# The causal mask mostly inside the second score product and the maxima product, mask products of 64 and 65 columns

## The reference

```python
q = apply_rotary_emb(q, cos, sin)
k = apply_rotary_emb(k, cos, sin)
scores = jnp.einsum('bhid,bhjd->bhij', q, k) * scale
scores = jnp.where(causal, scores, -jnp.inf)
probs = jax.nn.softmax(scores, axis=-1)
out = jnp.einsum('bhij,bhjd->bhid', probs, v)
```

## Time and profile before

| | |
|---|---|
| median of 3 runs | 1208.22 us (1207.09 to 1208.79) |
| profiled execution, its own time | 1207.18 us |
| its span in the trace | 1205.1 us |
| PE busy | 1128.8 us, 94% of the span, 13543 matmuls |
| DVE / ACT / POOL busy | 994.7 / 939.9 / 938.7 us |
| slots 1 to 14 in the trace | 130.1 to 896.0 us |
| last slot | to about 950 us, then the feed-forward part |

### The profile page before, as it was taken

How to read it: one execution, slowest core, us unless ns; L and a number is a source line. 1 busy time by engine, 2 the same in 40 slices (tenths; PEclk the granted TensorE clock), 3 DMA queues, 4 the chain that set the end, 5 groups by cost and what they waited for, 6 DMA issues and landing times. The chain is left out here.

```text
span 1205.1 us, 34913 instructions
## 1 busy us (share of the span) xinstructions
PE 1128.8 (94%) x13543; PEld 790.1 (66%) x13543; DVE 994.7 (83%) x2262; ACT 939.9 (78%) x2180; POOL 938.7 (78%) x980
## 2 busy tenths in 40 slices
PE   4689999999999999999999999999998788999996
PEld 1256677777767777777777777777776555566563
DVE  7799797888879797978879797879789579877987
ACT  3667988889797979789797979788898576656574
POOL 3468899999999999999989999999677445334463
PEclk8699999999999999999999999999999899999999
DMA  6651524262442515252534515152520100000011
GB/s 204 160 141 47 131 65 116 69 141 68 110 116 63 140 38 143 69 125 63 133 85 94 132 46 141 47 132 72 141 68 2 36 1 2 1 2 1 2 36 36
DMA packets 50660, 97.03 MB, mean 81 GB/s; under 512 B 6720, under 2 KB 23360, under 8 KB 48448
## 3 DMA queue, kind: packets, MB, share of 16 engines
q1 hardware_dynamic: 50496, 94.81, 31.5%
HBM read 58.47 MB, written 34.60 MB: 77 GB/s over the span
## 5 line engine op out<-in xcount | busy, mean ns | idle before, releaser
L847 POOL TENSOR_TENSOR Plo<-P,Phi 128x512 f16<-128x512 f32 (+3 forms) x640 | 538.1, 868 | 69.9 <-ACT P L516 66.7
L513 ACT ACTIVATE Phi<-psS 128x512 f16<-128x512 f32 (+3 forms) x768 | 392.5, 511 | 131.2 <-PE psS L368 83.2
L516 ACT ACTIVATE P<-psS 128x512 f32<-128x512 f32 (+3 forms) x640 | 315.1, 493 | 0.0
L392 PE MATMUL psO<-V,Plo 128*128 128x65 f16 x2304 | 288.4, 194 | 0.0
L388 PE MATMUL psO<-V,Phi 128*128 128x65 f16 x2304 | 287.1, 192 | 0.3 <-DVE On L805 0.3
L390 PE MATMUL psO<-V,Phi 128*128 128x64 f16 x2304 | 286.2, 192 | 0.0
L365 PE MATMUL psS<-Q,K 128*128 128x512 f16 (+3 forms) x768 | 251.6, 328 | 12.6 <-DVE Plo L672 9.5
L388 PEld LDWEIGHTS psO<-V,Phi 128*128 128x128 f16 x2304 | 219.7, 98 | 56.7 <-issue 1.0
L368 PE MATMUL psS<-Q,K 65*128 65x512 f16 (+3 forms) x768 | 252.3, 329 | 0.0
L721 DVE TENSOR_REDUCE pmax<-psX 128x1 f32<-128x512 f32 x384 | 242.8, 682 | 1.1 <-PE psX L452 0.6
L390 PEld LDWEIGHTS psO<-V,Phi 128*128 128x128 f16 x2304 | 213.9, 96 | 30.8
(11 more groups left out here) (194 smaller groups left out, 2175.8 us busy)
## 6 DMA issues: line engine op xcount, KB each, us to landing
K<-k_way SPq DMA_DIRECT2D x48, 512.0 KB, 6.9
k_way<-HL SPq DMA_DIRECT2D x64, 256.0 KB, 4.2
q_way<-HL SPq DMA_DIRECT2D x60, 256.0 KB, 3.9
Q<-q_way SPq DMA_DIRECT2D x60, 256.0 KB, 6.8
Q<-q_way SPq DMA_DIRECT2D x15, 512.0 KB, 11.7
out<-y SPq DMA_DIRECT2D x8, 256.0 KB, 2.2
y<-in_x SPq DMA_DIRECT2D x3, 512.0 KB, 10.9
Q<-HL SPq DMA_DIRECT2D x16, 64.0 KB, 4.8
```

What stands on the lines that cost most here:

```text
L392: mm = nc.tensor.matmul(O, M.Plo[:, U % NP_, k * P:(k + 1) * P], V[:, HD:2 * HD + 1], start=False, stop=j == t, skip_group_check=True)
L513: nc.scalar.activation(M.Phi[:, U % NP_, 0:w], X, ACT.Exp, scale=SCALE)
L516: nc.scalar.activation(full, X, ACT.Exp, scale=SCALE).then_inc(S.exp_done, 1)
L847: nc.gpsimd.tensor_tensor(M.Plo[:, U % NP_, 0:w], M.P32[:, U % NP_, 0:w], M.Phi[:, U % NP_, 0:w], ALU.subtract).then_inc(S.lo_pool, 1)
```

## The change

The idle rows 65 to 127 of `K2` and `Q2` get a constant pattern: row r of `K2` holds 32768 at key r of each block and 0 elsewhere, row r of `Q2` holds -32768 at the queries below r. Their product is a large negative number where the key is above the query, for keys 65 to 127 of a block. So the diagonal 128 columns are a product of all 128 rows, the other columns one of 65 rows, and a mask product is left for keys 0 to 64 alone: 64 query columns in the scores, 65 key columns in the maxima. The 65-row operands are now high against high: `K2` holds key high and `Q2` query high, `K1` key low and key high, `Q1` query high and query low. The maxima are taken from `K2` and `Q2` alone, without the term of the low keys, and row 64 of `Q2` is zeroed by a DMA ahead of them. The pattern is built by POOL in `Plo` and copied by ACT (16 copies of 64 x 1024 f16, `far_rows`) during the start. Two small DVE copies become reductions. `load(s)` still moves 3 MB in 8 DMAs, the first one being the row of zeros of 8 KB. The DMA of the row of 64.0 and its semaphore go.

```diff
 NEG = -1.0e30
 LOWEST = -3.0e38
 MSCALE = 64.0
+BIG = 32768.0
+LEFT = HD + 1
 VW = 2 * HD + 2
 E, TOPK, H = 8, 4, 128
 SH = 2 * H
 assert sorted((t, j + i) for bank in MAXB for t, j, n in bank for i in range(n)) == [
     (t, j) for t in range(TT) for j in range(t + 1)]
 LO_LAG = 0
+NEAR = (48, 32)
 LAG = 5
 NP_ = 6
 NS = 3
 MT_FIRST = ((-1, 17), (0, 1), (0, 11), (0, 19))
 MX_SECOND, JOIN_SECOND, MT_SECOND = (13, 41), 42, 44
 EARLY_STEPS = 12
+FAR_AT = {(-2, 2): (4, 5), (-2, 3): (6, 7), (-2, 6): (8, 9), (-2, 8): (10, 11), (-1, 20): (12, 13), (-1, 22): (14, 15)}
 X_SUM = {(-2, 8): 1, (-2, 10): 2, (-1, 2): 3}
 X_SQUARE = {(-1, 5): (1, 2), (-1, 17): (3,)}
 X_ROOT, X_RECIPROCAL = (-1, 19), (0, 6)
...
                 nc.tensor.matmul(out, M.K1[:, p, h, j * P:(j + 1) * P], M.Q1[:, p, h, c:c + w],
                                  start=True, stop=False)
 
-                mm = nc.tensor.matmul(out, M.K2[0:HD + 1, p, h, j * P:(j + 1) * P],
-                                      M.Q2[0:HD + 1, p, h, c:c + w], start=False, stop=not diagonal)
+                keys = slice(j * P, (j + 1) * P)
                 if diagonal:
-                    mm = nc.tensor.matmul(out[:, 0:P], M.ident16[:], M.maskT[:], start=False, stop=True)
+                    nc.tensor.matmul(out[:, 0:P], M.K2[:, p, h, keys], M.Q2[:, p, h, keys], start=False, stop=False)
+                    if w > P:
+                        nc.tensor.matmul(out[:, P:w], M.K2[0:LEFT, p, h, keys], M.Q2[0:LEFT, p, h, c + P:c + w],
+                                         start=False, stop=False)
+                    mm = nc.tensor.matmul(out[:, 0:HD], M.ident16[:], M.maskT[:], start=False, stop=True)
+                else:
+                    mm = nc.tensor.matmul(out, M.K2[0:LEFT, p, h, keys], M.Q2[0:LEFT, p, h, c:c + w],
+                                          start=False, stop=True)
                 mm.then_inc(S.scores_ready, 1)
 
             def weighted(U):
...
                                                   start=i == 0, stop=i == 2)
                 elif kind == "mx":
                     h, k = a
-                    if (s, h, k) == (-1, 1, 0):
-                        pe.wait_ge(S.first_twin, 16)
+                    if (s, h, k) == (-1, 0, 0):
+                        pe.wait_ge(S.far_rows, 2 * GH)
+                    if (s, h, k) == (0, 0, 0):
+                        pe.wait_ge(S.far_rows, 4 * GH)
                     if k == 0 and h % 2 == 0:
                         if s < 0:
                             pe.wait_ge(S.first_k, 32)
                             pe.wait_ge(S.first_q[h // 2], 16 * GH)
                         else:
-                            pe.wait_ge(S.near_in[h // 2], 48 * (s + 1))
+                            pe.wait_ge(S.near_in[h // 2], NEAR[h // 2] * (s + 1))
                     c = 0
-                    rows = HD if s < 0 and h == 0 else P
                     for t, j, n in MAXB[k]:
                         diagonal = j + n - 1 == t
-                        mm = nc.tensor.matmul(X[:, c:c + n * P], M.Q1[0:rows, p, h, t * P:(t + 1) * P],
-                                              M.K1[0:rows, p, h, j * P:(j + n) * P], start=True, stop=not diagonal)
-                        c += n * P
+                        plain = n - diagonal
+                        own = slice(t * P, (t + 1) * P)
+                        if plain:
+                            mm = nc.tensor.matmul(X[:, c:c + plain * P], M.Q2[0:LEFT, p, h, own],
+                                                  M.K2[0:LEFT, p, h, j * P:(j + plain) * P], start=True, stop=True)
+                        c += plain * P
                         if diagonal:
-                            mm = nc.tensor.matmul(X[:, c - P:c], M.ident16[:], M.maskN[:], start=False, stop=True)
+                            nc.tensor.matmul(X[:, c:c + P], M.Q2[:, p, h, own], M.K2[:, p, h, own],
+                                             start=True, stop=False)
+                            mm = nc.tensor.matmul(X[:, c:c + LEFT], M.ident16[:], M.maskN[:], start=False, stop=True)
+                            c += P
...
+            def far_rows(n):
+
+                p, k, h = n // (2 * GH), n // GH % 2, n % GH
+                rows = (M.K2, M.Q2)[k][HD:P, p, h].rearrange("p (t i) -> p t i", i=P)
+                pattern = M.Plo[HD:P, k, 0:P].rearrange("p (o i) -> p o i", o=1)
+                nc.scalar.copy(rows, pattern.to_broadcast([HD, TT, P])).then_inc(S.far_rows, 1)
+
...
+            act.wait_ge(S.patterns, 2)
+            for n in range(2):
+                far_rows(n)
             for k in range(2):
                 tiles = slice(k * HT, (k + 1) * HT)
                 act.wait_ge(S.var_ready[0], k + 1)
                 nc.scalar.activation(M.std[:, tiles], M.std[:, tiles], ACT.Sqrt).then_inc(S.std_ready[0], 1)
+            for n in range(2, 4):
+                far_rows(n)
             weight_hi(0)
             for s, u in steps:
                 U = SU * s + u
                 if s >= 0 and U <= last_unit:
                     exps(U)
+                for n in FAR_AT.get((s, u), ()):
+                    far_rows(n)
                 for item in act_at.get((s, u), []):
                     side(item)
...
-                nc.vector.tensor_copy(M.pmax[:, 1, h, 0:5:4], M.pmix[:, h, 0:2, 3]).then_inc(S.max_parts, 1)
+                nc.vector.tensor_reduce(M.pmax[:, 1, h, 0:5:4], M.pmix[:, h, 0:2, 3:4], AX.X, ALU.max).then_inc(S.max_parts, 1)
...
-                nc.vector.tensor_copy(M.pmax[:, 1, :, 0:5:4], M.pmix[:, :, 0:2, 3]).then_inc(S.max_parts, 1)
+                nc.vector.tensor_reduce(M.pmax[:, 1, :, 0:5:4], M.pmix[:, :, 0:2, 3:4], AX.X, ALU.max).then_inc(S.max_parts, 1)
...
             nc.gpsimd.memset(M.ident[:], 0.0)
             nc.gpsimd.memset(M.ident16[:], 0.0)
             nc.gpsimd.memset(M.maskT[:], 0.0)
-            nc.gpsimd.memset(M.maskN[:], 0.0).then_inc(S.consts, 1)
+            nc.gpsimd.memset(M.maskN[:], 0.0)
+            nc.gpsimd.memset(M.Plo[:, 0, 0:P], 0.0)
+            nc.gpsimd.memset(M.Plo[:, 1, 0:P], -BIG).then_inc(S.consts, 1)
             pool.wait_ge(S.consts, 1)
             for t in (M.ident, M.ident16):
                 nc.gpsimd.affine_select(out=t[:], in_=t[:], compare_op=ALU.not_equal, fill=1.0, base=0,
                                         pattern=[[-1, P]], channel_multiplier=1)
 
+            nc.gpsimd.affine_select(out=M.Plo[:, 0, 0:P], in_=M.Plo[:, 0, 0:P], compare_op=ALU.not_equal, fill=BIG, base=0,
+                                    pattern=[[-1, P]], channel_multiplier=1)
+            nc.gpsimd.affine_select(out=M.Plo[:, 1, 0:P], in_=M.Plo[:, 1, 0:P], compare_op=ALU.is_ge, fill=0.0, base=-1,
+                                    pattern=[[-1, P]], channel_multiplier=1).then_inc(S.patterns, 1)
+
             nc.gpsimd.affine_select(out=M.maskT[:], in_=M.maskT[:], compare_op=ALU.is_ge, fill=NEG, base=0,
-                                    pattern=[[1, P]], channel_multiplier=-1)
+                                    pattern=[[1, HD]], channel_multiplier=-1)
             nc.gpsimd.affine_select(out=M.maskN[:], in_=M.maskN[:], compare_op=ALU.is_ge,
-                                    fill=NEG, base=0, pattern=[[-1, P]], channel_multiplier=1).then_inc(S.consts, 1)
-            nc.gpsimd.memset(M.scale_row[:], MSCALE)
+                                    fill=NEG, base=0, pattern=[[-1, LEFT]], channel_multiplier=1).then_inc(S.consts, 1)
+            pool.wait_ge(S.patterns, 1)
+            for k, value in enumerate((MSCALE, 0.0)):
+                last = nc.gpsimd.affine_select(out=M.Plo[:, k, 0:P], in_=M.Plo[:, k, 0:P], compare_op=ALU.not_equal,
+                                               fill=value, base=-HD, pattern=[[0, P]], channel_multiplier=1)
+            last.then_inc(S.patterns, 1)
+            nc.gpsimd.memset(M.zeros[:], 0.0)
             nc.gpsimd.memset(M.eps[:], EPS)
             nc.gpsimd.memset(M.V[:, :, :, :, 2 * HD:2 * HD + 1].rearrange("p a t h o -> p (a t h) o"), 1.0)
             nc.gpsimd.memset(M.pmax[:], LOWEST).then_inc(S.consts, 1)
...
                                  M.HL[h * HALF:(h + 1) * HALF, 0, :, :]).then_inc(S.first_out, 16)
                 sp.wait_ge(S.first_out, 16 * GH)
                 for i in range(2):
-                    sp.dma_start(M.K1[:, 0, 2 * i:2 * i + 2], krows[:, 2 * i:2 * i + 2]).then_inc(S.first_k, 16)
-                sp.dma_start(M.K2[0:HD, 0], krows[0:HD]).then_inc(S.first_k2, 16)
+                    sp.dma_start(M.K2[0:HD, 0, 2 * i:2 * i + 2], krows[0:HD, 2 * i:2 * i + 2]).then_inc(S.first_k, 16)
+                sp.dma_start(M.K1[0:HD, 0], krows[HD:P]).then_inc(S.first_k1, 16)
+                sp.dma_start(M.K1[HD:P, 0], krows[0:HD]).then_inc(S.first_k1, 16)
 
             def first_queries():
 
...
                 for h in range(GH):
                     rows = slice(h * HALF, (h + 1) * HALF)
                     for k in range(2):
```

(21 more changed lines are left out.)

27 lines of the change are left out of this document (12 added, 15 removed).

## The result

The changed kernel takes 1199.24 us (median of 6 runs, 1197.42 to 1203.23) against 1208.47 for the kernel before on the same chips (6 runs, 1205.76 to 1210.03): a ratio of 0.9927, 95% interval 0.9907 to 0.9948. It is faster by 9 us, and the forecast was 16. The profiled execution has a span of 1196.8 us against 1205.1, at a mean granted clock of 0.98.

What follows compares the result with a forecast made beforehand. PE was taken to bound slots 1 to 14. Gains of 20.5 us, less 2.8 give-back and 1.6 start, leave 16.1 off 1207.2: 1191.1, as median 1192; own range 1186 to 1197, widened to 1186 to 1199.

Steps and rivals of the forecast that it cites:

- the start: Before slot 1: ACT's pattern copies and a second table load, less DVE's saved copies, cost a net 1.6 us.
- masks: PE's mask products in scores and maxima: narrowing saves 0.027 us each, 1.73 us per slot.
- splits: PE's diagonal products cut in two: 48 more matmuls a slot at 0.007 us, 0.34 us in all.
- give-back: Slots 1 to 14: waits on other engines return 0.2 us of PE's saving per slot, 2.8 us in all.
- 0.7 for slot 0: Slot 0: gains half of a steady slot's 1.39 us, 0.7 us.
- I let 0.8 of them lie on its path: DVE's L744 copies at the start: some 2 us saved, 0.8 counted as lying on DVE's path.
- the price of 0 for the loads: Operand loads: same 3 MB and 8 issues, arriving earlier for the maxima and as before for the scores, cost 0.
- A: Steady slots: POOL and the three banks of scores hold the slot near 53.9 us; gain 6.3 us, 1202; chance 0.14.
- B: Start: costs +4 us in place of +1.6, the copies' delay running through DVE's slot 0; 1194.5; chance 0.14.
- C: PE's splits: switching active rows exposes the next weight load, 98 ns per split, 71 us; slower at 1253; chance 0.03.
- D: PE's masks: a 64-column bf16 product takes as long as one of 128, so no gain; 1215; chance 0.03.
- The test I set: Steady slots of the changed profile: forecast 53.0 to 53.2 us; staying above 53.6 would mean the forecast is wrong.

Runs made afterwards that it cites:

- `wide_masks`: The changed kernel with both mask products, of scores and maxima, 128 columns wide as before; 1210.87 us against 1208.51 for the kernel before.
- `before_less_act`: The kernel before, with ACT's exponentials on 448 of 512 columns in 16 units of a slot; 1198.42 us against 1208.51 for the kernel before.
- `no_masks`: The changed kernel without its mask products in the scores and the maxima; 1193.91 us against 1207.26 for the kernel before.
- `less_pool`: The changed kernel with POOL forming the low half of only 448 of 512 columns in 16 units of a slot; 1197.75 us against 1207.26 before.

## Why the prediction failed by half

**The step that failed** is the term "I take 0.2 us in each of 14 slots, nearer to 0, since no wait of more than 0.7 us is there today". A steady slot gave back 1.34 - 0.52 = 0.82 us. The range for it (0 to 0.9) held the value; the choice inside it did not. With 0.82 in place of 0.2 the sum would have been 8.7 us smaller and the forecast 1200.7, beside 1199.24 measured. That this is so near is in part luck: the start came out 1.2 us better than forecast, slots 9, 10 and 13 gained 1.7 us more than a steady slot, and slot 14 gave 1.6 back.

The range was also stated too narrow. With the ends that the prediction gives for each term (masks 0.030 and 0.024, splits 0 and 0.01, give-back 0 to 6, start -0.5 to 2.5), all at once, the sum runs from 1179 to 1201 and not from 1186 to 1197.

Three readings led to the 0.2.

First, the stalls of the kernel before were not in the views I took them from. "Each matmul starts when the columns of the one before it have been streamed, with no gap between kinds of work" was true of the 1.66 us of the earlier trace rows and not of the slot: 0.85 us of stalls, the largest 0.21, were in its start-to-start distances, and the waits of the slot listed 0.4 us for `Plo`, 0.2 for `pmax` and 0.2 for `OT`. The waits of PE itself listed nothing, since they count from a modelled end.

Second, a small wait was read as a small risk. Where a wait is over zero, its releaser has no slack there, and what PE saves before it, back to the last place where the releaser itself waited for PE, is lost. Step 11 shows this to 0.01 us; the other stalls were not followed in this way. ACT's unbroken stretch begins 4.33 us after the slot's start (462.69 - 458.36) and 4.44 before the change (466.35 - 461.91): 0.11 us of PE's saving had reached it. The score product behind the stall starts 11.55 us after the slot's start (469.91 - 458.36), and 11.66 before (473.57 - 461.91): again 0.11. Everything that the masks saved in between went into the stall, 0.21 to 0.42. That is 0.21 of the 0.82 us.

Third, the total of an engine was taken for its limit. ACT with 46.2 and DVE with 45.1 us of 53.9 hold PE, POOL with 51.4 does not. The program says why. `scores` waits, before it refills a bank, for ACT's second exponential of unit `U - 3`, or for DVE's low half where DVE forms it from the bank itself (units 4 and 8 of 12). POOL reads a copy, and only `weighted` waits for it, five steps later. So PE can be ahead of ACT and DVE by three units at most. That this distance is the cause, and not only the place of the waits, was not tried: no run has another number of banks.

**Terms that held.** PE's stream lost 1.34 us in a slot against 1.39 forecast. Masks: 0.027 us each was forecast, and the stream of `wide_masks` is 1.59 us longer than that of the changed kernel, 0.025 for each of 64. Splits: 0.007 us forecast, 5 ns of stream and 4 ns of slot measured with `wide_masks`. The rule of the Trainium skill (TensorE: Matmul & The Clock Gate, Back-to-back issue gap) of 81 ns for a product of 128 columns in such a stream does not hold here, as argued: the f16 and bf16 products of 128 columns in slot 7 mostly follow each other at 55 to 60 ns. Its formula for a single one, columns over 2.4 GHz and 2.5 ns, gives 29 ns for 64 columns, where the trace shows 28 to 33.

**The start** was forecast at +1.6 us, less 0.7 for slot 0, so slot 1 at 0.9 later; it began 0.29 earlier. The second table load and the exponentials at 66 (65.75) are as forecast. From 60 to 90 us DVE did 24.64 us of work in place of 27.64, in part since its V waited 3.40 us for ACT's cast in place of 1.41, and from 90 to 120 it did 29.03 in place of 27.67: 3.0 us behind, 1.4 caught up. The rest may be what it no longer had to do. The reductions that replace the copies of `L744`:

```profile
L774 DVE TENSOR_REDUCE pmax<-pmix x4: 140/144/147, 50.3 to 94.9; 128x2 f32<-128x2 f32 x4
```

They take 140 to 147 ns where the four copies took 160 to 1010, so about 2 us leave DVE, and I let 0.8 of them lie on its path. Counted in full they bring the start term to +0.4, and slot 1 to 0.3 earlier, as measured. That is arithmetic on one execution of each kernel, in which the granted clock differs as well (0.84 for 0.90 from 60 to 90 us, 1.00 for 0.94 from 90 to 120), and by the spread above it is not shown: the copies were not put back alone. The agreement can be luck.

**Slot 14** lost 1.09 us, which no step foresaw. It ends with PE's wait for the row maxima: the transfer is issued at 884.41 and PE goes on at 888.11, 3.70 us later; before, PE went on 2.35 us after the issue (893.63 to 895.98). From the product before it, PE's first score product of slot 15 starts 1.50 us later in place of 0.12, so without this the slot would have gained 0.3 us. What delays the transfer is the code packet shown above, so the price of 0 for the loads is not refuted by it: `wide_masks`, with the new operands, and `before_less_act`, with the old ones, have the same delay there (1.19 and 0.61 us from the product before), and `no_masks`, with the new ones, has none there and 1.1 us at the head of slot 13. It also corrects a reading of the earlier trace rows. The 0.7 us wait there, at the head of slot 5, was put down to the start of a batch; three packets of that transfer begin at 350.88, where a code packet ends at 350.90. The kernel before has such a delay, 0.75 us, at the head of slot 11 that the changed one has not, and that is more than half of slot 10's gain of 1.25.

**The rivals.** A (followers bind, slot at 53.9) was right in the slot. It named POOL and the three banks: `less_pool` rules POOL out, and the waits that remain are on the banks of scores and of maxima. B (+4 at the start) has no support in a slot 1 that begins no later. C and D are refuted: 4 to 5 ns for a split, 0.03 us for a narrow mask. The test I set, "wrong if slots stay above 53.6 (A)", came true at 53.89.
